# A graph-attention kernel on one Trainium2 core: the masked maximum in four passes of 1024 columns a block where it was eight of 512

## What is computed

```
# layer 0: mean over the neighbours
mask = adj > 0;  agg = mask @ x / max(sum(mask), 1)
y    = relu(concat(x @ W_self + b_self, agg @ W_nb + b_nb) @ W_comb + b_comb)
x1   = layernorm(x + y)
# layer 1: attention over the neighbours
neib_att = tanh(neigh @ Wn1 + bn1) @ Wn2 + bn2
x_att    = tanh(x1 @ Wx1 + bx1) @ Wx2 + bx2
ws  = leaky_relu(x_att @ neib_att.T, 0.01)           # 4096 x 4096
ws  = softmax(where(mask, ws, -9e15), axis=1)
z   = concat(x1 @ Wfx + bfx, ws @ (neigh @ Wv + bv))
out = layernorm(x1 + z)
```

## Time and profile before

| | |
|---|---|
| median of 3 executions | 768.94 us (768.76 to 770.57) |
| the profiled execution | 770.73 us, of which 768.9 us from its first to its last instruction |
| granted TensorE clock, mean | 0.996 |
| busy: PE, DVE, ACT, POOL | 733.2, 610.5, 584.7, 125.3 us |
| L622, masked maximum | 256 passes, 176.2 us, and 256 reads of the accumulator, 20.7 us |
| chain that ended last, by engine | PE 87%, ACT 4%, DVE 3%, issue 3% |

### The profile page before, as it was taken

How to read it: one execution, slowest core, us unless ns; L and a number is a source line. 1 busy time by engine, 2 the same in 40 slices (tenths; PEclk the granted TensorE clock), 3 DMA queues, 4 the chain that set the end, 5 groups by cost and what they waited for, 6 DMA issues and landing times.

```text
span 768.9 us, 20264 instructions
## 1 busy us (share of the span) xinstructions
PE 733.2 (95%) x7536; PEld 631.0 (82%) x7536; DVE 610.5 (79%) x1563; ACT 584.7 (76%) x1078; POOL 125.3 (16%) x241
## 2 busy tenths in 40 slices
PE   5989989999999999999999999999999999999785
PEld 4646768888888888888888889888888888887564
DVE  4886477888888888888888888888888888877874
ACT  2455258888888888888888888888888888888995
POOL 0010120111111111111111111111111111111101
PEclk9999999999999999999999999999999999999999
DMA  8968997876677776676876668677667677620000
GB/s 266 363 151 163 220 246 172 179 173 148 157 150 175 176 180 158 158 156 161 180 179 150 160 164 159 167 180 172 138 171 163 170 179 174 122 43 8 8 9 14
DMA packets 175154, 120.43 MB, mean 157 GB/s; under 512 B 140368, under 2 KB 158672, under 8 KB 175056
## 3 DMA queue, kind: packets, MB, share of 16 engines
q1 hardware_dynamic: 174612, 119.11, 65.1%
q10 hardware_dynamic: 444, 0.02, 0.0%
HBM read 81.35 MB, written 4.19 MB: 111 GB/s over the span
## 4 chain that ended last, share of the span: by engine, by line
PE 87%; ACT 4%; DVE 3%; issue 3%; DMA 1%; POOL 1%; SPq 0%; POOLq 0%; ACTq 0%; DVEq 0%
PE ps_v L1036 20%; PE ps_t L1023 14%; PE ps_agg L999 14%; PE ps_agg L1002 14%; PE ps_agg L1056 7%; PE ps_s L1014 6%; PE ps_v L921 2%; PE ps_s L913 2%; PE ps_x L1073 1%; PE ps_x L1076 1%; ACT score L829 1%; DMA neigh_sb<-in_L_gnn_neigh_dram 1%; ACT score L822 1%; PE ps_x L930 1%; PE ps_t L904 1%
## 5 line engine op out<-in xcount | busy, mean ns | idle before, releaser
L999 PE MATMUL ps_agg<-x,mask_t 128*128 128x257 f16 x1024 | 239.7, 272 | 1.5 <-DMA mask_t<-mask 1.5
L1002 PE MATMUL ps_agg<-x,mask_t 128*128 128x256 f16 x1024 | 234.5, 272 | 0.0
L679 DVE TENSOR_TENSOR late<-ps_t,late 128x512 f16<-128x512 f32 x256 | 174.8, 683 | 74.2 <-ACT late L835 71.6
L1036 PEld LDWEIGHTS ps_v<-v,late 128*128 128x128 f16 x3072 | 189.9, 97 | 50.9 <-DVE late L679 16.6
L1036 PE MATMUL ps_v<-v,late 128*128 128x128 f16 x3072 | 213.5, 219 | 9.2 <-DVE late L679 6.7
L822 ACT ACTIVATE score<-ps_s,sc 128x512 f32<-128x512 f32 x256 | 178.0, 695 | 53.0 <-PE ps_s L1014 51.5
L622 DVE CUSTOM_DVE_ANT_0 score<-score,mask 128x512 f32<-128x512 f32 x256 | 176.2, 688 | 18.7 <-ACT score L822 17.2
L835 ACT CAST late<-ps_t 128x512 f16<-128x512 f32 x256 | 150.2, 587 | 15.2 <-PE ps_t L1023 15.1
L1023 PE MATMUL ps_t<-ident,score 128*128 128x128 f32 x1024 | 157.3, 276 | 3.4 <-ACT score L829 3.4
L829 ACT ACTIVATE score<-score,exp_bias,sc 128x1024 f32<-128x1024 f32 x128 | 158.7, 1240 | 1.6 <-DVE exp_bias L631 1.6
L1023 PEld LDWEIGHTS ps_t<-ident,score 128*128 128x128 f32 x1024 | 107.9, 141 | 6.8 <-ACT score L829 4.7
(11 more groups left out here) (125 smaller groups left out, 705.7 us busy)
## 6 DMA issues: line engine op xcount, KB each, us to landing
adj_sb<-in_adj_dram SPq DMA_DIRECT2D x128, 512.0 KB, 4.7
neigh_sb<-in_L_gnn_neigh_dram SPq DMA_DIRECT2D x8, 512.0 KB, 8.0
score<-in_x_dram SPq DMA_DIRECT2D x8, 512.0 KB, 8.5
x_in<-in_x_dram SPq DMA_DIRECT2D x32, 128.0 KB, 3.9
out_dram<-out_sb SPq DMA_DIRECT2D x32, 128.0 KB, 4.5
mask_t<-mask SPq DMA_TRANSPOSE x128, 4.2
mask<-in_L_gnn_W_comb_dram SPq DMA_DIRECT2D x1, 512.0 KB, 10.1
mask<-in_L_gnn_W_self_dram SPq DMA_DIRECT2D x1, 256.0 KB, 7.1
```

What stands on the lines that cost most here:

```text
L679: dve.tensor_tensor(p_lo[:, k % 2, :], ps_t[k % 2][:, :], p_hi[:, k % 2, :], ALU.subtract).then_inc(p_lo_made, 1)
L999: mm = pe.matmul(agg[:, 0:D + 1], mask_t8[:, c, 0, :], x16[:, c, 0:D + 1], start=(c == 0), stop=(c == NC - 1), skip_group_check=True)
L1002: mm = pe.matmul(agg[:, 0:D], mask_t8[:, c, 0, :], x16[:, c, X_LO:X_LO + D], start=False, stop=False, skip_group_check=True)
L1036: mm = pe.matmul(ps_v[:, 0:DV], p[:, k % 2, chunk], v16[:, c, v:v + DV], start=(c == 0 and part == 0), stop=(c == NC - 1 and part == 2))
```

## The change

`masked_scores` takes a quarter of 1024 columns instead of a group of 512. Its four passes stand in slots 0, 2, 4 and 6, two slots behind the leaky relu of the quarter's first group, one behind that of its second. `part_max` has four columns, and the two other waits on `score_made` count quarters. Everything else is as before.

```diff
-        part_max = sb("part_max", [P, NG], F32)
+        part_max = sb("part_max", [P, NQ], F32)
...
             def make_mask(b, q):
...
-                at_least(dve, score_made, NG * (b - MASK_BUFS) + 2 * q + 2)
+                at_least(dve, score_made, NQ * (b - MASK_BUFS) + q + 1)
...
-            def masked_scores(b, k):
-                dve.wait_ge(leaky_made, NG * b + k + 1)
-                dve.wait_ge(mask_made, NQ * b + k // 2 + 1)
-                part = slice(k * GW, (k + 1) * GW)
+            def masked_scores(b, q):
+                dve.wait_ge(leaky_made, NG * b + 2 * q + 2)
+                dve.wait_ge(mask_made, NQ * b + q + 1)
+                part = slice(q * QW, (q + 1) * QW)
                 dve.tensor_tensor_reduce(score[:, b % 2, part], score[:, b % 2, part], mask[:, b % MASK_BUFS, part],
                                          1.0, -3.0e38, ALU.subtract, ALU.max,
-                                         part_max[:, k:k + 1]).then_inc(score_made, 1)
+                                         part_max[:, q:q + 1]).then_inc(score_made, 1)
 
             def row_max(b):
-                dve.wait_ge(score_made, NG * (b + 1))
+                dve.wait_ge(score_made, NQ * (b + 1))
...
-                if d := due(s, SCORE_AT + 1):
-                    masked_scores(*d)
+                if (d := due(s, SCORE_AT + 2)) and d[1] % 2 == 0:
+                    masked_scores(d[0], d[1] // 2)
```

## The result

The changed kernel takes 788.18 us (median of 4 runs, 786.44 to 788.41) where the kernel before takes 768.85 in the same job: ratio 1.0242, 95% interval 1.0228 to 1.0256. It is slower, as forecast; 786.3 us was predicted, with a range of 780 to 792. The profiled execution of the changed kernel took 786.44 us, 784.6 of them from first to last instruction.

The account below looks back on a forecast made before the run. TensorE, busy 95% of the span, was taken to set the steady pace, with slot 0's VectorE chain reaching it without slack. Slot 0's 15.5, the first blocks' 0.5 and the end's 1.4 us added to 768.94 gave 786.3 us, range 780 to 792.

Parts of the forecast that it names:

- The price of the pass: VectorE's new pass over 1024 columns: 1.22 us by the slope of the SBUF reductions, 0.533 more than over 512.
- rival 3: Where TensorE is short of work, after 702 us: each pair of passes made one saves 0.24 us; 766.3 us, 5%.
- Slot 0 decides: VectorE's pass in slot 0 heads a chain without slack to TensorE: 29 blocks x 0.533 = 15.5 us.
- Two ends, L697 and the exponentials: Slot 0's chain reaches TensorE at slot 1's weight load (0.05 us slack at most) and slot 2's transposes (none).
- the freed slot 7 brings nothing: Slot 0's pass waits for the leaky relu done at 408.23; slot 7 without a pass lets it start no sooner.
- Slot 6 and slot 4, covers of under 0.1 us, cost nothing: Delays to slot 6's exponentials and slot 4's p_low stay covered, by 0.03 to 0.08 and at most 0.05 us.
- The first blocks: Only there TensorE waits for x1, which follows slot 4's later layer0: one step of 0.53 us added.
- The end phase: After 702 us exponentials wait for the row maximum 3 times, each 0.533 later, some 0.2 given back: 1.4 us.
- The sum: Whole kernel: 15.5 for slot 0, 0.5 for the first blocks and 1.4 for the end, 17.4 us.
- The upper bound: Upper bound of the main forecast's time: 29 x 0.56 with 3 at the ends, 788.5 us.
- Which side of the rule: For VectorE, at 79% and not saturated: larger operations delay other engines, so the time rises; slower 90%.

Follow-up runs that it names:

- a dose: One needless `bn_stats` over 256 columns a block on VectorE in slot 0, added to the kernel before: 779.33 us, 9.8 over it.

## Why the prediction was right, step by step

- **The price of the pass**, 1.22 us by the slope of the reductions: 1.220 us. The estimate that the text drew from the Trainium skill (VectorE: DVE Perf Modes, the section on the TRN2 errata) was 1.224. By the same formula 512 columns take, by estimate, 691 ns. Rows 3 have 688, so a row did bear on it. What a pair saves was overrated: the accumulator read starts together with the next instruction (both at 415.50), so a wide pass costs 1.15 us from start to start, a narrow one 0.62 (408.26 to 408.88 before), and a pair saves some 0.1 us, not the 0.24 of rival 3. That rival's sum didn't fit its condition either: with a pass of 0.74 us a pair would save 0.72 by the recorded durations.
- **Slot 0 decides.** Shown by the rows, by undoing it (766.02 and 764.28 us), by making only it (786.75) and by a dose (9.8 us for 28 x 0.33). Size: 28 blocks took 15.55 us more. 27 of them took 0.534 each, against the 0.533 forecast, and the first 1.14 (22.04 us against 20.90). That first one's extra 0.6 us was not forecast; it is gone where L697 is moved ahead (21.42 us), and its cause is open otherwise.
- **Two ends, L697 and the exponentials.** The exponentials' end is shown by moving L697: no gain. L697's end is read from the changed kernel's trace, where L1036 starts 0.52 us later. Its slack was 0.01, within the "0.05 us at most"; at the exponentials' end the slack was less than none, as the kernel before was already held 0.10 us a block there.
- **Slot 0's head: "the freed slot 7 brings nothing".** This was the weak sentence. It brings nothing to slot 0, but it absorbs slot 6's long pass; with slot 7's pass put back the head was 0.39 us late. The sum wasn't touched, as the change frees the slot.
- **Slot 6 and slot 4, covers of under 0.1 us, cost nothing.** Right in the changed kernel: no wait for the bias in the steady part. VectorE's p_low of slot 4 and bias of slot 6, ScalarE's exponentials of slot 7 and the weight load of slot 5 in the changed kernel (compare):

```profile
407.86 0.66 DVE L679 TENSOR_TENSOR late<-ps_t,late 128x512 f16<-128x512 f32 x1
...
411.50 0.21 DVE L631 TENSOR_SCALAR exp_bias<-row,sc 128x1 f32<-128x1 f32 x1
```

```profile
411.79 1.23 ACT L829 ACTIVATE score<-score,exp_bias,sc 128x1024 f32<-128x1024 f32 x1
```

```profile
408.58 0.88 PEld L1036 LDWEIGHTS ps_v<-v,late 128*128 128x128 f16 x12
```

  The bias is done at 411.71 and the exponentials start at 411.79 without idle time; p_low ends at 408.52 and the load goes at 408.58. What was misjudged is what lies behind slot 6: another 0.1 to 0.2 us that the leaky relu has.
- **The first blocks**: 0.53 for one late x1, and one chain of 0.53. Second to fourth mean gained 1.05, so the number came out, but the reason given for half of it did not. Slot 0's pass alone brings 1.02 there, with slot 4 narrow; with slot 4 wide and slot 0 narrow it is 0.08, although TensorE's wait for x1 rises to 2.3 us there. The x1 that slot 4 makes late cost next to nothing, and the two halves came out together by luck. In the changed kernel that wait rose from 1.8 to 2.6 us:

```profile
PE ps_x L1067 <- ACT x L841: 2.6, 3, 1.0
...
ACT score L829 <- DVE exp_bias L631: 2.4, 3, 1.2
```

- **The end phase**: 1.4 us forecast, 1.59 measured. The exponentials' wait for the bias rose by 0.8 us only, so the size came out better than its reason. The kernels with degrees first put 1.42 us on the last two quarters, those nearest the row maximum; but the kernel with only the first quarter narrow has the same wait of 2.4 us and loses 0.73 in this stage. Which of the late steps carries how much is open.
- **The sum**: 17.4 us forecast, 18.2 by the stages. The medians differ by 19.3. Of the four executions the one with a mean clock of 0.995 took 786.44 us, the three at 0.990 took 787.96 to 788.41. No trace of these three was kept, but the kernel with only the first quarter wide has 0.990 as well, and there the clock leaves its upper level (2.4 GHz) at the entry to the end phase (its stretches, columns as above):

```profile
710.00:715.00 5.00, 5.00 (x57) 4.52 (x56) 3.06 (x8) 4.40 (x8) 0.75 (x1) 1.00 0.00 2
715.00:720.00 5.00, 3.11 (x32) 2.39 (x31) 3.54 (x12) 3.17 (x7) 0.19 (x1) 0.91 0.00 0
720.00:725.00 5.00, 5.00 (x45) 4.74 (x44) 3.44 (x10) 4.04 (x9) 1.76 (x3) 0.75 0.02 5
```

  TensorE had been full until 715 and then had 1.9 us of idle time. In the changed kernel's own trace, at 0.995, the same stretch has the same 3.11 us of busy TensorE and the clock stays at 1.00, so the idle time alone doesn't decide it. The executions of the kernel with only the first quarter wide split in the same way: 785.83 and 786.05 us at 0.997 and 0.993, 787.45 and 787.61 at 0.990. That one to two microseconds of the median come from this is likely; no trace of one kernel in both states shows it.
- **The upper bound.** 29 x 0.56 + 3 is 19.2 us, so the forecast's own upper bound is 788.2 and not 788.5. The measured median stands on it.
- **Which side of the rule.** The prediction weighed the two rules of the Trainium skill (Perfetto Trace Analysis, Optimizing Scalar/DVE Operations), larger operations for a saturated engine against smaller ones where an engine idles others. The traces agree with the second, with a limit that they add: once degrees stands ahead of the pass, wide or narrow is worth 1.7 us, and the order is worth 22 with wide passes (788.18 to 766.02).

## What to carry to other kernels

Before widening an instruction on an engine with time to spare, follow what stands behind it in that engine's order to the first wait of the bound engine: the added length is paid in full, once a turn, if that chain has no slack, and where it has some, only what goes beyond it. Here the better edit was to move the head of the chain ahead of the long work: two lines, worth more than either width. A freed place elsewhere in the order is not useless because it frees nothing on the chain: it may be what keeps an earlier delay from reaching it.

## What the runs showed of the hardware

A record's duration is not what an instruction costs its engine: `bn_stats` over 256 columns is recorded with 0.42 us, costs 0.46 from start to start when the next one waits for its result, and 0.33 when nothing does. A needless instruction put into the 0.12 us that a reduction waits for the accumulator's write is free to that extent. An accumulator read is recorded with 0.08 us but starts together with the next instruction, and adds nothing from start to start unless that one needs its result. And where the weight load stood idle, it began 0.05 to 0.06 us after p_low's end (418.84 to 418.89 with L697 moved), and 0.11 to 0.12 after L697's.
